# A routed-expert block on one core: POOL's gathers and scatters lose the wait between them and are written in one merged order, and the second expert product is written one step later

## The reference, cut to what matters

```python
x = x + 0.5 * moe(layernorm(x), Wr, br, W1, b1, W2, b2)   # layer 0
x = x + mamba(layernorm(x), ...)
x = x + 0.5 * moe(layernorm(x), Wr, br, W1, b1, W2, b2)   # layer 1

def moe(x, Wr, br, W1, b1, W2, b2):                        # 8 experts, 128 -> 512 -> 128
    logits = xt @ Wr + br
    top_vals, top_idx = jax.lax.top_k(logits, 2)
    ...
    h = jax.nn.relu(jnp.einsum('td,edh->teh', xt, W1) + b1)
    y = jnp.einsum('teh,ehd->ted', h, W2) + b2
    out = jnp.einsum('ted,te->td', y, gate)
```

## Time and profile before

| | us |
|---|---|
| median of 3 runs | 422.05 (419.68 to 422.75) |
| the profiled execution | 421.09 |
| its span, first to last instruction | 419.3 |
| PE busy | 330.8 (79%) |
| DVE busy | 269.0 (64%) |
| POOL busy | 220.7 (53%) |
| ACT busy | 209.8 (50%) |

### The profile page before, as it was taken

How to read it: one execution, slowest core, us unless ns; L and a number is a source line. 1 busy time by engine, 2 the same in 40 slices (tenths; PEclk the granted TensorE clock), 3 DMA queues, 4 the chain that set the end, 5 groups by cost and what they waited for, 6 DMA issues and landing times.

```text
span 419.3 us, 8909 instructions
## 1 busy us (share of the span) xinstructions
PE 330.8 (79%) x2366; PEld 294.6 (70%) x2366; DVE 269.0 (64%) x920; ACT 209.8 (50%) x501; POOL 220.7 (53%) x263
## 2 busy tenths in 40 slices
PE   8784799986698198799999999749469998778800
PEld 7684799976697185567777779739459998767700
DVE  4883477753465178768788986899447775345416
ACT  3832456644464065736657573453245665455402
POOL 4026355566545177274656879651644556654512
PEclk9578899999899598899999999877899999899965
DMA  6791111111111410000000000010111111111154
GB/s 161 239 283 45 27 39 42 40 44 44 41 33 33 172 48 2 1 0 2 1 2 3 0 0 2 2 74 28 52 31 39 38 41 45 41 40 38 33 172 147
DMA packets 18674, 22.23 MB, mean 53 GB/s; under 512 B 4114, under 2 KB 13508, under 8 KB 18628
## 3 DMA queue, kind: packets, MB, share of 16 engines
q1 hardware_dynamic: 13092, 11.18, 8.9%
q0 software_dynamic: 4096, 8.40, 6.7%
q10 hardware_dynamic: 1440, 2.11, 1.4%
HBM read 14.33 MB, written 7.34 MB: 52 GB/s over the span
## 4 chain that ended last, share of the span: by engine, by line
PE 51%; DVE 11%; issue 9%; DMA 6%; SPq 6%; ACT 5%; POOL 4%; another core or an unknown queue 3%; DVEq 3%; ACTq 0%; POOLq 0%
PE PS L793 16%; PE PS L805 16%; SPq L401 3%; PE PS L842 3%; PE PS L849 3%; PE PS L896 2%; PE PS L814 2%; PE PS L778 2%; DMA YT_all<-y_rows 2%; SPq L395 2%; DMA y_rows<-YS,rows_out 2%; DVE X L1507 2%; POOL rs L501 2%; DVE YT_all L1475 1%
## 5 line engine op out<-in xcount | busy, mean ns | idle before, releaser
L479 POOL DMA_INDIRECT XG<-xn_rows,rows_in x64 | 62.1, 970 | 83.8 <-issue 35.7
L793 PE MATMUL PS<-XT_all,W1B 128*128 x624 | 90.1, 290 | 15.8 <-DVE XT_all L1454 8.0
L793 PEld LDWEIGHTS PS<-XT_all,W1B 128*128 128x128 f32 x624 | 80.3, 201 | 18.9 <-issue 18.2
L1121 ACT ACTIVATE H<-PS,W1B 128x128 f32<-128x128 f32 x156 | 48.7, 363 | 88.9 <-PE PS L793 60.7
L489 POOL DMA_INDIRECT y_rows<-YS,rows_out x64 | 62.3, 974 | 48.3 <-issue 18.9
L805 PE MATMUL PS<-H,W2B 128*128 128x128 f32 x624 | 85.3, 281 | 0.5 <-issue 0.5
L805 PEld LDWEIGHTS PS<-H,W2B 128*128 128x128 f32 x624 | 78.4, 197 | 0.9 <-issue 0.6
L1484 DVE COPY W2B<-W2S 128x513 f32 x78 | 35.5, 455 | 39.1 <-DVE YT_all L1475 26.6
L1111 ACT ACTIVATE W1B<-W1S 128x516 f32 x78 | 49.4, 633 | 21.7 <-issue 9.0
L1475 DVE TENSOR_SCALAR YT_all<-PS,W2B 128x128 f32 x78 | 27.2, 349 | 43.3 <-PE PS L805 25.8
L1465 DVE TENSOR_SCALAR H<-PS,W1B 128x128 f32<-128x128 f32 x156 | 46.9, 342 | 6.4 <-PE PS L793 3.8
(11 more groups left out here) (204 smaller groups left out, 556.0 us busy)
## 6 DMA issues: line engine op xcount, KB each, us to landing
YT_all<-y_rows SPq DMA_DIRECT2D x8, 512.0 KB, 5.1
W1S<-in_L_ffn_W SPq DMA_DIRECT2D x1, 2048.0 KB
W2S<-in_L_ffn_W SPq DMA_DIRECT2D x8, 256.0 KB
xn_rows<-XN ACTq DMA_DIRECT2D x8, 256.0 KB, 4.4
X<-in_L_attn_x SPq DMA_DIRECT2D x4, 256.0 KB, 4.7
XG<-xn_rows,rows_in POOLq DMA_INDIRECT x64
y_rows<-YS,rows_out POOLq DMA_INDIRECT x64
out_x<-X SPq DMA_DIRECT2D x4, 256.0 KB, 2.3
```

Source lines behind the costliest of these rows:

```text
L479: g.indirect_dma_start(out=XG[:, u, :], out_offset=None, in_=xn_dram, in_offset=bass.IndirectOffsetOnAxis(ap=rows_in[:, i:i + 1], axis=0), ...
L793: last = mm(PS[2 + 2 * half + j % 2][:, c * P:(c + 1) * P], W1B[w][:, h * P:(h + 1) * P], XT_all[:, ds(start, P)], start=True, stop=True)
L1121: last = A(H[w][:, 2 + c, :], PS[4 + j % 2][:, c * P:(c + 1) * P], ACT.Relu, bias=W1B[w][:, HID + 2 + c:HID + 3 + c])
```

## The change

Three edits, all in `experts`.

1. POOL's transfers no longer raise `s_issued` and no longer wait for it.
2. POOL's gathers and scatters are written in one loop over the steps: 8 gathers, then for each step s the gathers of tile i + 8 for each tile i that arrives in s, and the scatters of the tiles that leave in s - 1.
3. PE writes, in step s, up(s + 1), the arrivals of s, the leaves of s - 1 and down(s - 1). DVE's bias, its copy of the second weights and ACT's copies out move by the same step.

```diff
-            def transfer_written():
-                nonlocal written
-                if written:
-                    pool.wait_ge(s_issued, written)
-                written += 1
-
...
-                for i in range(DENSE):
+                def gather(i):
                     u = i % XG_RING
                     if i >= XG_RING:
                         pool.wait_ge(s_xt, layer * len(ARRIVALS) + GROUP_OF[i - XG_RING] + 1)
-                    transfer_written()
                     g.indirect_dma_start(out=XG[:, u, :], out_offset=None, in_=xn_dram,
...
-                for m, tiles in enumerate(LEAVES):
+                def scatter(m):
                     pool.wait_ge(s_ysc, layer * len(LEAVES) + m + 1)
...
+                for i in range(XG_RING):
+                    gather(i)
+                for step in range(-2, SLOT_TILES + 2):
+                    for a in arrivals_at(step):
+                        for i in ARRIVALS[a]:
+                            if i + XG_RING < DENSE:
+                                gather(i + XG_RING)
+                    for m in leaves_at(step - 1):
+                        scatter(m)
...
@@ PE @@
-                    if step < SLOT_TILES - 1:
-                        for m in leaves_at(step):
-                            leave(m)
-                    if step >= 0:
-                        down(step)
+                    for m in leaves_at(step - 1):
+                        leave(m)
+                    if step >= 1:
+                        down(step - 1)
+                down(SLOT_TILES - 1)
...
@@ DVE @@
-                    if step >= 0:
-                        add_bias(step)
-                        if step + TRIO < SLOT_TILES:
-                            second_weights_of(step + TRIO)
+                    if step >= 1:
+                        add_bias(step - 1)
+                        if step - 1 + TRIO < SLOT_TILES:
+                            second_weights_of(step - 1 + TRIO)
+                add_bias(SLOT_TILES - 1)
```

More of the change, by code:

```diff
@@ L295, in macaron_block @@
         s_w2 = sem("s_w2")
-        s_issued = sem("s_issued")
         s_upa = sem("s_upa")
@@ L458, in _ @@
             g.iota(iota_a[:], pattern=[[1, DENSE], [0, NG]], base=0, channel_multiplier=0, **small).then_inc(s_iota, 1)
-            written = 0
-            def transfer_written():
-                nonlocal written
-                if written:
-                    pool.wait_ge(s_issued, written)
-                written += 1
             def experts(layer):
@@ L477, in experts @@
                         pool.wait_ge(s_xt, layer * len(ARRIVALS) + GROUP_OF[i - XG_RING] + 1)
-                    transfer_written()
                     g.indirect_dma_start(out=XG[:, u, :], out_offset=None, in_=xn_dram,
-                                         in_offset=bass.IndirectOffsetOnAxis(ap=rows_in[:, i:i + 1], axis=0),
-                                         engine_sem=s_issued
+                                         in_offset=bass.IndirectOffsetOnAxis(ap=rows_in[:, i:i + 1], axis=0)
                                          ).then_inc(s_gath[u], 16)
-                for m, tiles in enumerate(LEAVES):
+                def scatter(m):
                     pool.wait_ge(s_ysc, layer * len(LEAVES) + m + 1)
-                    for i in tiles:
+                    for i in LEAVES[m]:
                         u = i % YS_RING
-                        transfer_written()
                         g.indirect_dma_start(out=y_dram, in_=YS[:, u, :], in_offset=None,
-                                             out_offset=bass.IndirectOffsetOnAxis(ap=rows_out[:, i:i + 1], axis=0),
-                                             engine_sem=s_issued
+                                             out_offset=bass.IndirectOffsetOnAxis(ap=rows_out[:, i:i + 1], axis=0)
                                              ).then_inc(s_sc[u], 16)
+                for i in range(XG_RING):
[7 more added lines that the diff above has]
+                        scatter(m)
             def add_output(k, g_, gated):
@@ L1142, in experts @@
                         weights_of(step + 3)
-                    if step < SLOT_TILES - 1:
-                        for m in leaves_at(step):
-                            copy_out(m)
+                    for m in leaves_at(step - 1):
+                        copy_out(m)
                 for m in leaves_at(SLOT_TILES - 1) + leaves_at(SLOT_TILES):
```

## The result

The changed kernel took 431.53 us (median of 4 runs, 429.6 to 433.81), the kernel before beside it 420.87 (4 runs, 415.56 to 422.75): ratio 1.0335, 95% interval 1.0213 to 1.0457. It is slower. Measured again later on another chip, on which the kernel before took 403.7, the same code took 389.22, ratio 0.9637 (0.9613 to 0.966): faster. Both are measured. I call the chip of the first eight experiments the first chip (before: 424), those of the other four the second (402.8) and the third (403.7).

The account below looks back on a forecast made before the run. PE was taken as the bound, its signals held up while POOL's transfers stand closer than some 1.5 us. Terms summed to +3.4 us a layer, twice +6.8 on 421.1: 428 us predicted, range 395 to 441 (8 in 10).

Parts of the forecast that it names:

- burst and lag: Opening gathers denser without the wait, +1.1 us a layer; first down a step later no longer covers a copy, +1.0.
- pairs: Steps 4 to 9: gathers come two together with each arrival, little of it shows; +1.0 us a layer, 0 to 7.9.
- new dense stretch: Steps 10 to 16: 16 transfers back to back, four leaves wait 3.0 us each; +12.0 us a layer, 0 to 14.8.
- scatters' block: Scatters no longer stand as 16 behind all gathers, so the old slow stretch ends; -9.5 us a layer.
- tail: End of layer: last scatters follow each other at shorter gaps; -2.2 us a layer, between -0.9 and -2.7.
- The prediction's sign of being wrong: If the four leaves in steps 10 to 16 wait under 1 us each, the kernel is faster instead.
- The sign for it: Denser opening gathers would show as steps 0 to 5 taking 17 us or more.
- The gap: Between POOL's transfers with one wait or none left: 0.30 us or less, with 0 as the other end.
- the likeliest case: The prediction's own sum, +3.4 us a layer, 428 us; covers 420 to 438, chance 0.40.
- Slower by much: Steps 4 to 16: the removed wait was all that kept PE's signals moving; +12.4 us a layer, 446 us, chance 0.10.
- The first rival: Spread scatters break up the long run, dense transfers cost PE nothing; 399.7 us, 388 to 412, chance 0.27.
- The collision of VectorE's copies with transfers: Denser POOL transfers hold every VectorE weight copy for 0.94 us, over 78 steps; 452 us, chance 0.03.

Follow-up runs that it names:

- paced kernels: Kernel before with an extra fulfilled wait ahead of each pair's second scatter (0.9977), or opening gathers too (0.9993); the change with its wait back and such waits (1.0047).
- the experiment with late leaves: Kernel before with PE's leaves and ScalarE's copies out one step later in their orders; 422.18 us, ratio 0.9969.
- The version with the memset: Kernel before without its wait between transfers, with a 128x128 memset of POOL ahead of each transfer instead; 385.22 us, ratio 0.9555.

## Why the prediction was right, and where it was lucky

The time (431.5 against 428, within 395 to 441) and the side (slower, 0.46) came out. Step by step, as the mean of the two layers, from the pace table for layer 0 and the same rows of layer 1 (us after the layer's first gather, in the kernel before and in the change: bias of step 5 at 27.1 and 29.7, of step 10 at 37.3 and 44.0, 20 at 58.6 and 72.2, 30 at 87.2 and 93.3, 38 at 105.1 and 109.8, last scatter 108.9 and 111.6):

| term | predicted | measured |
|---|---|---|
| burst and lag, up to step 5 | +1.1 +1.0 | +3.2 |
| pairs, steps 5 to 10 | +1.0 | +3.5 |
| new dense stretch, steps 10 to 20 | +12.0 | +7.4 |
| scatters' block, steps 20 to 30 | -9.5 | -8.5 |
| steps 30 to 38 | 0 | -0.1 |
| tail | -2.2 | -1.8 |
| layer | +3.4 | +3.7 |

Twice 3.7, and 1.0 between the layers, is 8.4 of the 8.5 us by which the span grew.

The nearness of 3.7 to 3.4 is luck in good part. The dense stretch came out 4.6 us a layer under its term, and the other terms together 4.9 over theirs. The luck has a second part, the chip, which the prediction did not consider.

- **The place and the mechanism** were right on the chip measured: the slow stretch vanished where it was and came in steps 10 to 17, with leaves that waited up to 4.57 us. The paced kernels show the mechanism: same work, wider spacing, signals on time, and PE through with step 38 at 92.5 us instead of 107.4.
- **The dense stretch** was sized too high, 12.0 against 7.4. I priced the four leaves of iterations 10, 12, 14 and 16 at 3.0 us. In layer 0 they waited 0.63, 0, 4.57 and 0 us, in layer 1 0.66, 0, 1.94 and 0.25: 4.0 a layer in place of 12.0. The rest of the loss came at places that had no price: the next leave of layer 0 (1.81) and arrivals (1.31, and 2.67 and 1.46 in layer 1). The prediction's sign of being wrong, four leaves under 1 us each, would have misled, for six of the eight were, and the kernel was slower. The unit was wrong: the experiment with late leaves shows that where the leaves stop waiting, PE waits elsewhere. The arrivals of layer 1:

```profile
341.59 0.44 PE L775 MATMUL PS<-ident,XG 128*128 128x128 f32 x2 [2.67 <-DVE XT_all L1450]
...
355.47 0.44 PE L775 MATMUL PS<-ident,XG 128*128 128x128 f32 x2 [1.46 <-DVE XT_all L1450]
```

- **The pairs** were sized too low by 2.5 us. I took them as harmless because the scatter pairs after 113 us were. Those have a pause behind each pair, 2.87 us in the earlier trace rows. Once the wait is gone the gathers of steps 4 to 9 stand 1.25 us apart in a pair, and the next pair starts 1.5 to 2.2 us behind the second of them, where the scatters' next pair starts 2.87 + 0.97 = 3.84 us behind. The run without the wait alone has the same pairs and the same cost (12.9 us in place of 10.2), so the merged order has no part in it. Whether the pairing or the mean spacing costs, no run tells apart.
- **Burst and lag** came to 3.2 instead of 2.1. The lag by itself is (1.5 + 3.3) / 2 = 2.4 of it, where I had 1.0. The term of 1.1 for a denser burst had no ground: the gaps there stay at 0.30, and the eighth gather starts 8.94 us after the first, where it was 9.20. The sign for it (steps 0 to 5 in 17 us or more) failed too: they took 12.52 by the downs, 57.59 - 45.07, and what was lost was lost before step 0, whose bias came 3.4 us later.
- **The gap** without any wait is 0.30 us, the same as with one. The lower end of 0 that I kept open is excluded; only where two waits stood together did a gap become shorter.
- **The tail** was right in size, -1.8 for -2.2.
- **One end of a sum.** For the likeliest case I gave 420 to 438. With leaves at 2.35 and no cost of pairs and burst, the sum is -9.5 + 9.4 + 1.0 - 2.2 = -1.3 a layer, 418.5 us and not 420. It changes nothing in the forecast.
- **The rivals.** "Slower by much, the wait was what kept the signals moving" was nearer the truth of the single part than I gave it credit for: the wait is worth 1.9% of 424 us by itself. Its 0.10 stands, since the sum stayed far from its 446. The first rival, in which dense transfers cost PE nothing, predicted 399.7 us and got 0.27; on the third chip its premise holds, and there the change gains 14.5 us. The collision of VectorE's copies with transfers did not happen: they take 443 ns at the mean after the change and 455 before, and 430 at the median in both. Before, and after:

```profile
L1484 DVE COPY W2B<-W2S 128x513 f32 x78 | 35.5, 455 | 39.1 <-DVE YT_all L1475 26.6
...
L1480 DVE COPY W2B<-W2S 128x513 f32 x78 | 34.5, 443 | 39.9 <-DVE YT_all L1471 25.6
```

The forecast was therefore right for its mechanism on one chip, and wrong in its sign on the third; on the second the change was not run. The prediction took the late signals as a property of the kernel; they are one of the kernel and the chip together. Nothing in the profile of before, which is of one chip, could show that, and 0.27 for the fast rival was all that covered it.

## What stays open

What differs between the chips isn't shown, nor by what path a transfer of POOL holds up a signal of PE. The ends of PE's rows are modelled, so it is open too whether a late signal waits behind finished work or whether the end of the work itself, the write of its result, comes late. The transfers' durations and gaps are the same, and PE's signals are on time on the first chip too where transfers stand 1.69 us apart. The kernel before was not traced on the second and third chips, so its 403 us there is explained by argument only: its POOL chain, 8 x 1.25 + 24 x 1.69 + 32 x 1.50 = 98.6 us a layer, would be the bound with PE free, 12 less than the 110.6 measured; twice 12 is 24, and the difference is 19 to 21. Nor was a spacing between 1.50 and 1.69 us run on the first chip, and there only added waits made the spacing wider: that the time between transfers counts, and not the waits as such, is argued and not shown. The version with the memset is known to beat the kernel before on the second chip only (385.22 against 402.79), and the change by a comparison across chips (ratio 0.9555 against 0.9637 on the third).

## What to carry to other kernels

Where an engine's results reach the others late only while another engine sends many small transfers, look at the distance between the starts of the transfers, and change that alone before any order. A faster issuing engine is a gain only until it takes away what the others need, and a paced one only until it is itself the bound: work out both chains to the end of the layer and take the later. And measure a change of a few per cent on more than one chip: here the kernel before itself differed by 5% between chips.

## What the hardware showed that I had not expected

- The same program took 424 us on one chip and 403 on two others, and a change to it was 3.35% slower by the one measurement and 3.6% faster by the other.
- On the first chip PE's signals fell up to 9.28 us behind with transfers 1.28 us apart, and were on time (0.56 at most) in the two kernels with 1.69 or more. The Trainium skill (SBUF — State Buffer, "Who interferes with whom") says that "PE and ACT never wait on anyone". That section is about the engines' ports into SBUF, and the prediction read it as a rule on signals, which it does not state. Read so, no kernel here would show a late signal; the second and third chips agree (0.57 at most), the first does not.
- VectorE's and ScalarE's signals stayed on time (0.02 us) beside the same transfers that held up PE's.
- A transfer of POOL follows another by 0.30 us whether it has a fulfilled wait or none, by 0.75 with two, and by 0.22 + 0.17 = 0.39 around a memset of 128x128: a memset in place of two waits is the shorter spacer (1.36 us from start to start against 1.69 to 1.72).
